# A graph network kernel whose one-hot picks stream 104 columns instead of 13

## What is computed

```python
msgs = z[edge_dst] @ Wd + z[edge_src] @ Ws + edge_weight[:, None] * ww[None, :] + bm
agg = jax.ops.segment_max(msgs, edge_dst, num_segments=n)      # 0 where a node has no edge
hidden = relu(z @ W1a + agg @ W1b + b1);  x = layernorm(x + hidden @ W2 + b2)
# then two mean aggregations over the same edges
mean = segment_sum(x[src], dst) / max(deg, 1)
h = relu(mean @ W1l.T + b1l + x @ W1r.T);  x = layernorm(x + conv2(h))
```

## Time and profile before

| what | value |
|---|---|
| median of three runs | 1476.27 us (1471.65 to 1479.07) |
| the profiled execution | 1471.77 us, its span 1469.7 us |
| mean granted clock of TensorE | 0.740 of full |
| TensorE matmul busy | 1183.3 us, 81% of the span |
| VectorE, GpSimd, ScalarE busy | 847.4, 775.9 and 408.5 us |
| the loop over the groups | about 60 to 1290 us of the span |

### The profile page before, as it was taken

One profiled execution on the slowest core, in us unless ns is written; L12 is line 12 of the kernel. 1 busy time (PEld: TensorE's weight loads), 2 busy tenths in 40 slices (PEclk: granted clock), 3 DMA queues, 4 the chain that ended last, 5 costly groups with the idle time before them and its releaser, 6 DMA issues.

```text
span 1469.7 us, 24820 instructions
## 1 busy us (share of the span) xinstructions
PE 1183.3 (81%) x6646; PEld 883.2 (60%) x6677; DVE 847.4 (58%) x3070; ACT 408.5 (28%) x1248; POOL 775.9 (53%) x828
## 2 busy tenths in 40 slices
PE   3798877988697887668798878878769678889998
PEld 3566656766575664556465666555556455665676
DVE  4455556665556655655655656566565555564455
ACT  2222222222222222222222222223222222221365
POOL 4555565665566556655665655565655555500132
PEclk8655566556758767866868567779668878899999
DMA  6322232223223323322332323332334322434521
GB/s 148 97 62 59 67 73 64 71 76 77 72 71 66 86 70 88 68 72 75 83 88 66 75 67 95 81 85 67 71 75 105 87 68 64 112 92 115 151 58 46
DMA packets 118181, 118.04 MB, mean 80 GB/s; under 512 B 23463, under 2 KB 102659, under 8 KB 118035
## 3 DMA queue, kind: packets, MB, share of 16 engines
q1 hardware_dynamic: 91110, 64.18, 17.2%
q0 software_dynamic: 24864, 50.97, 14.7%
q10 hardware_dynamic: 2061, 1.20, 0.3%
HBM read 103.60 MB, written 12.68 MB: 79 GB/s over the span
## 4 chain that ended last, share of the span: by engine, by line
PE 53%; another core or an unknown queue 19%; issue 10%; DVE 7%; ACT 4%; SPq 3%; DMA 3%; ACTq 2%; DVEq 0%
PE bank L1536 12%; PE bank L1539 8%; PE bank L1523 6%; PE bank L1718 5%; PE bank L1482 5%; PE bank L1587 4%; PE bank L1555 3%; PE bank L1470 3%; ACT area L789 2%; DVE area L1090 2%; DVE area L1110 2%; PE bank L1542 2%; ACTq L774 1%; DVE area L1091 1%
## 5 line engine op out<-in xcount | busy, mean ns | idle before, releaser
L924 POOL DMA_INDIRECT area<-zs_d,area x757 | 726.7, 960 | 512.9 <-PE bank L1482 201.3
L1110 DVE TENSOR_TENSOR_SCAN area<-area,bank 128x512 f32<-128x512 bf16 x196 | 249.9, 1275 | 395.1 <-PE bank L1482 225.6
L1536 PE MATMUL bank<-area 128*128 128x13 f32 x1564 | 306.5, 310 | 197.6 <-ACT area L789 148.9
L1536 PEld LDWEIGHTS bank<-area 128*128 128x128 f32 x1564 | 293.5, 263 | 244.0 <-ACT area L789 170.3
L781 ACT CAST adj_w<-bank 128x325 f32 x391 | 175.6, 449 | 858.2 <-PE bank L1542 451.8
L1090 DVE TENSOR_SCALAR area<-area 128x128 bf16<-128x128 f16 x782 | 216.1, 276 | 110.7 <-remote 83.6
L1091 DVE TENSOR_SCALAR area<-area 128x325 bf16<-128x325 f16 x782 | 248.0, 317 | 0.0
L1539 PE MATMUL bank<-area 128*128 128x325 bf16 x782 | 227.1, 383 | 0.3 <-issue 0.3
L1523 PE MATMUL bank<-ident,area 128*128 128x128 f32 x782 | 174.1, 364 | 0.0
L1482 PE MATMUL bank<-ident,area 128*128 128x128 f32 x762 | 160.4, 346 | 0.0
L1587 PE MATMUL bank<-adj_w,area 128*128 128x512 bf16 (+4 forms) x494 | 119.3, 384 | 28.9 <-DVE area L1122 9.2
(11 more groups left out here) (166 smaller groups left out, 1002.9 us busy)
## 6 DMA issues: line engine op xcount, KB each, us to landing
area<-mask_d SPq DMA_DIRECT2D x195, 128.0 KB
area<-zs_d,area POOLq DMA_INDIRECT x757
area<-zs_d SPq DMA_DIRECT2D x640, 0.5 KB
area<-wp_d SPq DMA_DIRECT2D x585, 3.0 KB
area<-parts_d SPq DMA_DIRECT2D x20, 384.0 KB, 7.8
zr_d<-area SPq DMA_DIRECT2D x24, 128.0 KB
area<-zr_d SPq DMA_DIRECT2D x6, 512.0 KB, 3.9
area<-scale_d SPq DMA_DIRECT2D x11, 256.0 KB, 4.1
```

Source lines behind the costliest of these rows:

```text
L924: pool.indirect_dma_start(gring[:, g % GR * 4 + s % 2 * 2 + u, :], None, x if g < RAW else zs_d[0:N, :], bass.IndirectOffsetOnAxis(ap=src_ ...
L1110: nc.vector.tensor_tensor_scan(S[:, g % 2, 0:n], mask[:, g % MR, 0:n], T_BANK[g % 2][:, 0:n], S[:, (g + 1) % 2, 511:512] if g else 0.0, AL ...
L1536: nc.tensor.matmul(o[:, 384:384 + W], St[:, b * P:(b + 1) * P], sel[:, g % 2, u, s % 2, :], start=u == 0, stop=u == 1)
```

## The change

The moving operand of the L1536 matmuls, 13 columns of `sel`, is read eight times over through an access pattern whose middle dimension has step 0, so that each matmul streams 104 columns. They are written to columns 384 to 487 of the bank, which has 512. The readers still take columns 384 to 396, which hold the same numbers as before. Nothing else is touched.

```diff
+WIDE = 8
...
                         for u in range(2):
                             b = s % 2 * 2 + u
-                            nc.tensor.matmul(o[:, 384:384 + W], St[:, b * P:(b + 1) * P], sel[:, g % 2, u, s % 2, :],
+                            nc.tensor.matmul(o[:, 384:384 + WIDE * W].rearrange("p (n w) -> p n w", w=W), St[:, b * P:(b + 1) * P],
+                                             sel[:, g % 2, u, s % 2, :].unsqueeze(1).broadcast_to([P, WIDE, W]),
                                              start=u == 0, stop=u == 1)
```

## The result

The changed kernel takes 1452.59 us (median; 1449.58 to 1458.63), the kernel before 1476.97 us in the same comparison: ratio 0.9845, with a 95% interval of 0.9803 to 0.9888. It is faster by 24 us, under half of the 56 us of the forecast, and inside its range. The profiled execution is the longest of those of after, 1458.63 us (span 1456.4), 13.1 us under the profiled one of before; its clock is the lowest of the four seen (0.827, 0.836, 0.838 and 0.845 went with 1458.6, 1454.4, 1450.7 and 1449.6 us).

A forecast was written before the change was run, and what follows sets the result against it. GpSimd's beat of 6.13 us a group was taken to bound the loop, with TensorE's clock costing only in fuller slots. Gains of 36 + 20 = 56 us off the median of 1476.3 gave 1420 us; range 1378 to 1474.

The forecast's parts named there:

- The bound: Loop over edge groups: GpSimd's beat of four gathers and a wait for held TensorE signals, 6.13 us a group.
- The direct cost: L1536 matmuls: 91 more columns hidden by the weight load, between 0 and 0.005 us an instruction, taken as 0.
- Rival 3: L1536 matmuls: added columns not covered by the weight load, so slower, about 1525 us; chance 0.10.
- The clock: TensorE in the loop: mean clock rises from 0.71 to about 0.88, and long low stretches go.
- The count slots: GpSimd's waits in 24 slots with degree counts fall from 3.4 to 1.9 us, gaining 36 us.
- The other 40 us, half taken as 20: Excess GpSimd waits in low-clock slots with values and roots or half pieces: 40 us, of which 20 us gained.
- Waits behind double bursts: About 38 GpSimd waits after gathers run on without a wait: 40 us of excess stays whatever the clock.
- The tail: Stretch after the loop, holding none of the changed instructions worth speaking of: unchanged.
- Rival 1: Loop: clock rises but only some count slots gain, 5 to 25 us, about 1460 us; chance 0.10.
- Rival 2: TensorE in the loop: clock doesn't rise, stays at 0.71, and nothing changes, 1476 us; chance 0.10.

The follow-up runs named there:

- e1: Kernel before (13 columns) with the fourth gather of every loop group left out, against the kernel before: 1260.43 us, ratio 0.8514.
- e9: The changed kernel again, on a chip that does not hold TensorE's signals, against the kernel before there: 1171.19 us, ratio 0.9968.
- e3: Kernel before (13 columns) with 2 of the 25 count matmuls of each tile, against the kernel before: 1449.26 us, ratio 0.9801.
- e4: Changed kernel (104 columns) with 2 of the 25 count matmuls of each tile, against the kernel before: 1445.13 us, ratio 0.9807.
- e16 to e18: Wide stream only in picks directly ahead of a count, only in all other picks, and the changed kernel; against the kernel before: 0.9844, 0.9914, 0.9836.
- e18: The changed kernel again, on another chip that holds the signals, against the kernel before there: 1435.45 us, ratio 0.9836.

## Why the forecast was wrong, point by point

- **The bound**: right. GpSimd's beat with held signals sets the loop: e1 took a gather away and got 1.18 of its 1.25 us back with TensorE's clock at 0.77.
- **The direct cost**: taken at 0, at most 0.005 us an instruction. It is 0.29 us a group at the low level and 0.13 at the high one, over 8 instructions 0.04 and 0.02. The step that failed took the start to start of L1581, which the picks at 128 columns were to resemble, as the bound for all. Three of four intervals do match it; the first, and at the low level the adjacency matmul behind, do not. Why the first alone grows was not tried. Rival 3's point of decision was 0.036 us an instruction on slots that TensorE ends. In plain slots 0.95 us of slack takes the cost up. The Trainium skill, page "TensorE: Matmul & The Clock Gate", section "The mechanism" of Part 3, lets a weight load overlap a running matmul only in another row group, though a sentence before that it names the background weight buffer as a second case. The rule of the row group alone is still not borne out: by it 91 more columns would have been paid in each of the four intervals, and three are unchanged.
- **The clock**: 0.81, not 0.88. The mechanism was right, and where the signals are not held it goes to 0.91 (e9). What was mis-sized is the share of time in which TensorE is idle behind double bursts; there the stream can't act, and the slot after is cold, as from 190 to 196 us above. That this makes up all of the missing 0.07 was not tried. (The forecast also read 8 and 9 tenths in the last five slices of the page; all five are 9.)
- **The count slots**: 36 us forecast, 18 measured in the pair. The warm wait was right (1.9 forecast, 1.76 measured), and so was the place (e3 with e4, e16 to e18). The failing step is that all 24 would be warm: 23 fall into the loop, 16 of them ran at the full level and 14 had the short wait. The mean wait of the nine others even stayed at 4.0 us (3.75 for the 19 long ones of before).
- **The other 40 us, half taken as 20**: nothing in the pair (242.2 to 243.7). It is the second mis-sized term, and the larger miss. The profile of after is that of its slowest execution; e18's, of the same program on another chip, has 234.4 there and 53.1 behind the counts, 8 and 26 us under before and still short of the 20 and 36 forecast, and the kernel before took 16 us less on that chip too. The direct cost of 0.13 to 0.29 us in each slot that TensorE ends can have eaten a part; this was only argued. e4 less e3, 4 us in the medians, tells how little is to be had without counts.
- **Waits behind double bursts**: as before, as forecast; 39 became 36.
- **The tail**: forecast as unchanged; from the last scan to the end 165.7 before, 171.3 after. With 18.3 us gained in the loop and under a microsecond from its start, this gives the 13.3 us of the two spans. The 5.6 us are not the change's: e18's trace, of the same program, has 165.5 from the last scan to the end.
- **Rival 1** (only some of the count slots gain, about 1460) was the nearest in mechanism and at 5 to 25 us also in size; its sign, waits still above 300 us with the clock up, came in at 300.1. Rival 2 fell, since the clock rose in every kernel. Rival 3's direct cost exists, but at a fourth of its price.

## What to carry to other kernels

Ask of a low clock which waits of the bounding queue depend on it, one kind of slot at a time, before pricing it: TensorE won 75 us of busy time and the loop 18. A stream that is widened for the clock acts only where the engine has work; where it was idle behind another queue's burst, for 6.63 us in the stretch above, the clock fell anyway, and the next full slot ran at 0.50. The interval between like instructions hid a cost at the joints here, 0.10 us in the first of four: take the whole block from first instruction to next piece of work.

## What the hardware showed that was not expected

- The same program took 1461 to 1477 us on some chips and 1173 to 1177 us on others. In the traces of the first kind TensorE's signals that fall into an unbroken burst of indirect gathers appear, in some eight of ten cases, 1.9 to 3.0 us after the start of the last gather, which is after its end (188.2 to 188.5 us above, for matmul ends from 180.5 on and a last gather from 185.43); in those of the second kind they appear 0.014 us after the matmul's end. What sets a chip to one or the other stays open.
- 104 fp32 columns instead of 13 left three of four intervals between matmul starts at 0.21 us (low level) and 0.11 us (high level) and lengthened the first to 0.32 and 0.17 us.
- Two bf16 matmuls of 325 columns behind the wide picks start 0.27 us apart at the low level instead of 0.23, and unchanged, 0.14 us, at the high one.
